# A logarithm from ScalarE's own function, and loads in another order, in a kernel of two wavefront scans and 128 attention images

## What is computed

```python
# L0 and L3: a scan over the cells of a spiral from the middle outwards
def step(g, inp):
    ci, ni, nm, nc = inp                        # cell, its up to 4 neighbours, mask, count
    local = g[:, ci, :]
    neigh = (g[:, ni, :] * nm[None, :, None]).sum(axis=1) / nc
    u = jnp.concatenate([local, neigh], axis=-1)
    y_sc = jnp.tanh(u @ w1 + b1) @ w2 + b2
    return g.at[:, ci, :].set(local + y_sc[:, None] * w_y[None, :]), None

# L1 and L2: attention of the 1024 cells of an image among themselves
q = x @ Wq + bq; k = x @ Wk + bk; v = x @ Wv + bv        # q and k have 16 channels
attn = softmax(q @ k.T)                                   # 1024 x 1024 per image
out = (gamma *) attn @ v + x
```

## Time and profile before

| | |
|---|---|
| runs | 4778.52 us median of 3 (4757.96 to 4780.98) |
| profiled execution | 4771.76 us, span from first to last instruction 4769.6 us |
| mean granted TensorE clock | 0.980 |
| scan 0, attention, scan 1 (by TensorE's first products) | from 13 us, from 816 us, from 3997 us |
| packets under 512 bytes | 443408 of 496962 |

### The profile page before, as it was taken

One profiled execution on the slowest core, in us unless ns is written; L12 is line 12 of the kernel. 1 busy time (PEld: TensorE's weight loads), 2 busy tenths in 40 slices (PEclk: granted clock), 3 DMA queues, 4 the chain that ended last, 5 costly groups with the idle time before them and its releaser, 6 DMA issues.

```text
span 4769.6 us, 56934 instructions
## 1 busy us (share of the span) xinstructions
PE 4486.8 (94%) x17064; PEld 2312.6 (48%) x17064; DVE 3579.9 (75%) x6748; ACT 2850.4 (60%) x5225; POOL 2278.8 (48%) x3972
## 2 busy tenths in 40 slices
PE   5999996999999999999999999999999798999997
PEld 2456754444444444444444444444444343446754
DVE  3888876777777777777777777777777574888876
ACT  1223322777777777777777777777777574223322
POOL 3454431455555555555555555555555455454431
PEclk7999998899999999999999999999999899999998
DMA  9569415111111111111111111111111515379625
GB/s 155 54 74 127 91 31 56 48 57 57 57 57 57 52 53 55 57 57 56 57 57 57 53 54 54 55 57 57 57 57 57 108 53 96 36 75 127 86 53 45
DMA packets 496962, 309.85 MB, mean 65 GB/s; under 512 B 443408, under 2 KB 446736, under 8 KB 496656
## 3 DMA queue, kind: packets, MB, share of 16 engines
q1 hardware_dynamic: 496656, 306.21, 32.7%
HBM read 137.34 MB, written 135.27 MB: 57 GB/s over the span
## 4 chain that ended last, share of the span: by engine, by line
PE 69%; POOL 14%; DVE 6%; issue 6%; SPq 2%; DMA 1%; ACT 1%; DVEq 0%; POOLq 0%; ACTq 0%
PE psum L983 14%; PE psum L925 9%; PE psum L916 8%; PE psum L906 8%; PE psum L954 7%; POOL probs_low L571 7%; PE psum L991 4%; PE psum L967 4%; PE psum L989 3%; PE psum L988 3%; PE psum L1024 3%; PE psum L1002 3%; PE psum L1011 3%; SPq L411 1%; DVE shared L711 1%
## 5 line engine op out<-in xcount | busy, mean ns | idle before, releaser
L571 POOL TENSOR_TENSOR probs_low<-shared,probs_high 128x512 fp32r<-128x512 f32 x1024 | 1307.9, 1277 | 1387.9 <-DVE probs_high L786 1387.9
L748 DVE TENSOR_REDUCE top<-psum 128x1 f32<-128x1024 f32 x1024 | 1253.5, 1224 | 596.8 <-PE psum L967 596.6
L852 ACT ACTIVATE shared<-psum 128x512 f32<-128x512 f32 x2048 | 1108.9, 594 | 376.0 <-PE psum L954 375.8
L857 ACT ACTIVATE psum<-psum,top 128x1024 f32<-128x1024 f32 x1024 | 1114.3, 1088 | 311.0 <-DVE top L748 311.0
L983 PE MATMUL psum<-shared 128*128 128x512 f32 x2048 | 1127.4, 632 | 3.3 <-DVE x L805 0.7
L842 ACT ACTIVATE shared<-psum,b_col 128x320 f32<-128x320 f32 (+10 forms) x744 | 413.3, 566 | 1101.5 <-PE psum L916 1086.5
L562 POOL TENSOR_TENSOR shared<-arena 128x32 f32<-128x32 f32 (+6 forms) x1230 | 570.6, 494 | 870.4 <-PE psum L916 802.6
L988 PE MATMUL psum<-probs_high,v_high 128*128 128x512 f32 x1024 | 813.1, 794 | 0.0
L906 PE MATMUL psum<-arena,w_own 128*128 128x320 f32 (+12 forms) x1672 | 543.3, 453 | 42.2 <-DMA arena<-x_cells 38.3
L916 PE MATMUL psum<-shared,w_sum 128*128 128x320 f32 (+10 forms) x1488 | 529.4, 478 | 42.1 <-POOL shared L562 28.4
L786 DVE CAST probs_high<-shared 128x512 fp32r<-128x512 f32 x1024 | 538.8, 526 | 21.3 <-ACT shared L852 21.3
(11 more groups left out here) (71 smaller groups left out, 4094.8 us busy)
## 6 DMA issues: line engine op xcount, KB each, us to landing
x<-layer_out SPq DMA_DIRECT2D x128, 512.0 KB, 3.2
layer_out<-x SPq DMA_DIRECT2D x128, 512.0 KB, 2.6
q<-q SPq DMA_DIRECT2D x256, 128.0 KB, 2.3
arena<-x_cells SPq DMA_DIRECT2D x8, 1520.0 KB, 10.4
layer_out<-arena SPq DMA_DIRECT2D x8, 1520.0 KB, 19.3
arena<-layer_out SPq DMA_DIRECT2D x8, 1520.0 KB, 10.7
y_cells<-arena SPq DMA_DIRECT2D x8, 1520.0 KB, 20.4
arena<-x_cells SPq DMA_DIRECT2D x4, 1504.0 KB, 18.8
```

The costliest lines, as they stand in the source:

```text
L571: nc.gpsimd.tensor_tensor(probs_low[n % 2][:], probs[u % PROBS], probs_high[n % 2][:], ALU.subtract).then_inc(probs_split, 1)
L748: nc.vector.reduce_max(top[i % 2][:, m:m + 1], rows_ps[m % 2][:], AX_X, negate=True).then_inc(row_max, 1)
L852: nc.scalar.activation(probs[u % PROBS], keys_ps[u % 2], ACT.Exp).then_inc(probs_ready, 1)
L857: nc.scalar.activation(rows_ps[m % 2][:], rows_ps[m % 2][:], ACT.Exp, bias=top[i % 2][:, m:m + 1], accum_out=total[i % 2][:, m:m + 1]).the ...
```

## The change

Five edits.

1. **The logarithm.** ScalarE takes Ln of the sums itself, then exp(-guess) as before; `guess_log` on VectorE is gone. GpSimd forms top - guess, then subtracts (shrink x sum - 1): 6 operations instead of 12. `LOG_TURNS` falls from 11 to 5.
2. **Chunks.** They start at levels 0, 2, 6, 8, 14, 20, 27, 34, 43, 53, 65, 80 and 101, now 13 beside `ENDING`. What isn't a ring's end ends at level 113 (`TAIL` = 114): chunk 12 has 38 cells, and the cells of levels 114 to 121 are counted to `ENDING`, now 28 cells. The arena keeps 512 columns.
3. **Loads by need.** At the start SyncE issues chunks 0, 1, ENDING and 2 of A, the same of B, then 3 to 6 of A and of B. ScalarE's queue issues the weights of both scans.
4. **First images.** During scan 0, behind the store of chunk 11, columns 0 to 957 (`OPEN`) of the images 0 to 3 are loaded; ScalarE copies their last 66 columns from the arena when the scan has ended.
5. **Images read back one by one.** Each image's columns 0 to 482 (`KEPT`) and its `ENDING` chunk are loaded into the arena in two DMAs after its last store, at s == 6 between `place_shift` and `swap_queries`; ScalarE copies those of the last image from x. `first_loads` is gone in both places.

```diff
-WINDOW = 5 * CHUNK - 16
+TAIL = 114
+WINDOW = 452
...
-    first = [0, 2]
-    for lv in range(2, LEVELS):
+    first = [0, 2, 6, 8]
+    for lv in range(8, TAIL):
...
+def wait_loaded(engine, n, g, k, loaded, refilled, last_filled):
+    if n == 0 or k not in FIRST_LOADS:
+        engine.wait_ge(loaded[g][k], 16 * (n + 1))
+    else:
+        engine.wait_ge(refilled[g], 32 * (IMAGES - (g == B)))
+        if g == B:
+            engine.wait_ge(last_filled, 2)
...
+FIRST_LOADS = sorted((k for k in range(NC) if not earlier_tenants(k)),
+                     key=lambda k: (min(FIRST_READ[chunk_cells(k)]), -chunk_size(k) if k else -CELLS))
+KEPT = sum(chunk_size(k) for k in FIRST_LOADS if k != ENDING)
+OPEN = STARTS[CHUNKS[ENDING - 1]]
...
+        def load_first_images():
+            for k in range(ENDING - 1):
+                sp.wait_ge(stored[A][k], 16)
+            for i in range(DEEP):
+                sp.dma_start(x[i][:, 0:OPEN], inner[0][i, :, 0:OPEN]).then_inc(x_in[i], 16)
+
+        def refill(i):
+            if is_job(i) and job_layer(i) == LAYERS - 1 and i < JOBS - 1:
+                g, b = i // (LAYERS * IMAGES), job_image(i)
+                sp.wait_ge(out_stored[i % DEEP], 16 * (i // DEEP + 1))
+                first = PLACES[0]
+                sp.dma_start(arena[:, b, first:first + KEPT], inner[LAYERS][b, :, 0:KEPT]).then_inc(refilled[g], 16)
+                sp.dma_start(arena[:, b, chunk_places_of(ENDING)], inner[LAYERS][b, :, chunk_cells(ENDING)]
+                             ).then_inc(refilled[g], 16)
...
+                if (n, what, k) == (0, "store", ENDING - 2):
+                    load_first_images()
...
-            load_scan_weights(0)
-            first_loads(0, A)
-            load_scan_weights(1)
-            first_loads(0, B)
+            for part in (FIRST_LOADS[:4], FIRST_LOADS[4:]):
+                for g in (A, B):
+                    for k in part:
+                        load(0, g, k)
...
                     if s == 6:
                         place_shift(j + 1)
+                        refill(j - 1)
...
-                if j == EARLY:
-                    first_loads(1, A)
             for b in range(DEEP):
                 sp.wait_ge(out_stored[b], 16 * (JOBS // DEEP))
-            first_loads(1, B)
...
-        def log_sums(i):
+        def shift_values(i):
...
+            pool.wait_ge(guess_ready, i + 1)
+            nc.gpsimd.tensor_tensor(log_sum[:], top[i % 2][:], guess[i % 2][:], ALU.subtract).then_inc(log_turn, 1)
             pool.wait_ge(shrink_ready, i + 1)
+            nc.gpsimd.tensor_tensor(ratio[:], shrink[i % 2][:], total[i % 2][:], ALU.mult).then_inc(log_turn, 1)
+            pool.wait_ge(log_turn, turn + 2)
+            nc.gpsimd.tensor_scalar(ratio[:], ratio[:], -1.0, None, ALU.add).then_inc(log_turn, 1)
+            pool.wait_ge(log_turn, turn + 3)
+            nc.gpsimd.tensor_tensor(ratio[:], log_sum[:], ratio[:], ALU.subtract).then_inc(log_turn, 1)
+            pool.wait_ge(log_turn, turn + 4)
...
         def shrink_sums(i):
             if is_job(i):
+                act.wait_ge(row_summed, MT * (i + 1))
+                nc.scalar.activation(guess[i % 2][:], total[i % 2][:], ACT.Ln).then_inc(guess_ready, 1)
                 act.wait_ge(guess_ready, i + 1)
...
+        def fill_first_images():
+            for i in range(DEEP):
+                for k in (ENDING - 1, ENDING):
+                    nc.scalar.activation(x[i][:, chunk_cells(k)], arena[:, i, chunk_places_of(k)], ACT.Copy
+                                         ).then_inc(x_tail, 1)
+
+        def fill_last_picture():
+            i = JOBS - 1
+            first = PLACES[0]
+            act.wait_ge(out_ready, 2 * i + 1)
+            nc.scalar.activation(arena[:, job_image(i), first:first + KEPT], x[i % DEEP][:, 0:KEPT], ACT.Copy
+                                 ).then_inc(last_filled, 1)
...
             pe.wait_ge(x_in[i % DEEP], 16 * (i // DEEP + 1))
+            if i < DEEP:
+                pe.wait_ge(x_tail, 2 * (i + 1))
```

More of the change, by code:

```diff
@@ L213 @@
 TOP_ROW = 54
-EARLY = JOBS - 12
 LN2 = math.log(2.0)
@@ L340, in network @@
     shrink = [sb(f"shrink{n}", [P, MT]) for n in range(2)]
[L341 to L342 removed]
+    ratio, log_sum = (sb(n, [P, MT]) for n in ("ratio", "log_sum"))
     shift = [sb(f"shift{n}", [P, 2 * MT], F32R) for n in range(2)]
@@ L369, in network @@
     scan_weights_ready = sem("scan_weights_ready")
+    refilled, last_filled, x_tail = [sem(f"refilled{g}") for g in range(GROUPS)], sem("last_filled"), sem("x_tail")
     loaded = [[sem(f"loaded{g}_{k}") for k in range(NC)] for g in range(GROUPS)]
@@ L490, in place_shift @@
                                  shift_row[i % 2][:, cells_of]).then_inc(shift_placed[i % 2], 16)
[L492 to L495, removed]
         def follow(n):
@@ L572, in split_probs @@
                                         ).then_inc(probs_split, 1)
-        def log_sums(i):
+        def shift_values(i):
             if not is_job(i):
                 return
-            s, y, e = total[i % 2], guess[i % 2], shrink[i % 2]
+            turn = LOG_TURNS * i
             high, low = shift[i % 2][:, 0:MT], shift[i % 2][:, MT:2 * MT]
-            turn = LOG_TURNS * i
+            pool.wait_ge(guess_ready, i + 1)
+            nc.gpsimd.tensor_tensor(log_sum[:], top[i % 2][:], guess[i % 2][:], ALU.subtract).then_inc(log_turn, 1)
@@ L793, in low_values @@
                                         ).then_inc(v_ready, 1)
-        def guess_log(i):
-            if is_job(i):
-                dve.wait_ge(row_summed, MT * (i + 1))
-                nc.vector.tensor_scalar(guess[i % 2][:], total[i % 2][:].bitcast(mybir.dt.int32), LN2 / 2.0**23,
-                                        -(127.0 - 0.043) * LN2, ALU.mult, ALU.add).then_inc(guess_ready, 1)
         def output(i, h):
@@ L880, in attention, with load_scan_weights @@
                 values(j + 1, s // 2)
+        def load_scan_weights(n):
+            w1, b1, w2, b2, w_y = scan_weights[n]
+            act.dma_start(w1_own[n][:], w1[0:P, :]).then_inc(scan_weights_in[n], 16)
+            act.dma_start(w1_sum[n][:], w1[P:2 * P, :]).then_inc(scan_weights_in[n], 16)
+            with nc.allow_non_contiguous_dma(reason="small weight columns"):
+                act.dma_start(b1_col[n][:], b1.rearrange("(h p) -> p h", p=P)).then_inc(scan_weights_in[n], 16)
+                act.dma_start(w2_col[n][:], w2.rearrange("(h p) -> p h", p=P)).then_inc(scan_weights_in[n], 16)
+                for h in range(HALVES):
+                    act.dma_start(w2wy[n][h][:], w_y.rearrange("(a c) -> a c", a=1).to_broadcast([P, P])
+                                  ).then_inc(scan_weights_in[n], 16)
+                act.dma_start(wy_col[n][:], w_y.rearrange("(c a) -> c a", a=1)).then_inc(scan_weights_in[n], 16)
+                act.dma_start(b2wy[n][:], b2.to_broadcast([P, 1])).then_inc(scan_weights_in[n], 16)
+        def fill_first_images():
+            for i in range(DEEP):
+                for k in (ENDING - 1, ENDING):
+                    nc.scalar.activation(x[i][:, chunk_cells(k)], arena[:, i, chunk_places_of(k)], ACT.Copy
[6 more added lines that the diff above has]
+                                 ).then_inc(last_filled, 1)
+            act.wait_ge(out_ready, 2 * i + 2)
+            nc.scalar.activation(arena[:, job_image(i), chunk_places_of(ENDING)], x[i % DEEP][:, chunk_cells(ENDING)],
+                                 ACT.Copy).then_inc(last_filled, 1)
+        load_scan_weights(0)
+        load_scan_weights(1)
         act.wait_ge(scan_weights_in[0], 16 * 8)
```

54 lines of the change are left out of this document (14 added, 40 removed).

## The result

| | median us | range | executions |
|---|---|---|---|
| before | 4778.23 | 4757.96 to 4780.98 | 4 |
| after | 4835.37 | 4833.05 to 4838.11 | 4 |

The account below looks back on a forecast made before the run. TensorE was taken as the bound, busy 4486.8 of 4769.6 us, so only its idle time could go. Gains 90 + 27.6 + 19.4 + 27 + 13.7 + 10.1 - 1.3 = 186.5 us gave 4589 us, range 4560 to 4656.

Parts of the forecast that it names:

- The logarithm: Attention stage: TensorE's wait for probs_low goes, gaining 90 us; two extra table loads in all cost 1.3 us, bounds 0 and 4.
- what would show it: Signs listed beforehand; wrong in kind if ScalarE shows hundreds of table loads or TensorE waits for ScalarE in the steady stage.
- rival 1: Attention: logarithm's set lacks the exponential, two table loads per image, 328 us; 5002 us fully exposed, 4838 half; chance 0.08.
- the other terms: Start, first scan to attention, early loads, second scan's start and end: gains of 97.8 us together, without the logarithm.
- The size of the logarithm's gain: Attention: 90 us of the 93.2 us wait for probs_low, 3 us coming back; bounds 45 and 96.
- rival 2: Attention: probs_low's wait is replaced by an equal one for ScalarE or VectorE, a ring of four engines; 4675 us, chance 0.09.
- The start: First scan: B's third chunk load comes seventh in the queue, TensorE starts at 38.7 us, 27.6 earlier; bounds 20 and 36.
- From the first scan to the attention: First images read during the scan's tail gain 20.4 us, less 1 for the swap queued behind stores (bounds 0 and 5): 19.4.
- rival 3: Stage edges: small chunk loads as slow as large ones, swap and stores collide, other terms halve; 4633 us, chance 0.08.
- The early loads: Attention at image 116: seven chunk loads and TensorE's standstill of 25.48 us go; gain 27 us, bounds 24 and 28.
- The start of the second scan: B's sums follow A's at once, so B's product comes 12.7 us earlier, plus 1 us: gain 13.7, lower bound 10.
- The end: After the last update two stores remain instead of four, 12.6 us instead of 22.7: gain 10.1 us, bounds 6 and 13.

Follow-up runs that it names:

- one_set: The kernel after with one table load placed by hand, ahead of the attention, of the set serving exponential and logarithm: 4587.75 us, ratio 0.9593 to before.
- table of stores: No scan or attention, only loads and stores of 4096 short rows, one at a time, at chosen columns and lengths: stores landed in 4.5 to 14.1 us.
- align: The kernel after with an ENDING chunk of 32 cells (992 to 1023) instead of 28, and chunk 12 of 34: 4797.01 us, ratio 1.0031 to before.
- edges_only: The kernel after with the old logarithm (VectorE's guess, GpSimd's 12 operations), so edits 2 to 5 alone: 4718.73 us, ratio 0.9866 to before.
- one_load: one_set with one more table load of the same set per image, ahead of the logarithm: 4667.88 us, ratio 0.9768 to before.

## Why the prediction was wrong, step by step

**The logarithm: the step that failed.** The sentence was: "If the tables are changed only where they must be, there are two more", priced at 1.3 us. There are 256 in the stage, one ahead of each logarithm and one ahead of the exponential behind it, and "what would show it" had named both signs that came: hundreds of table loads, and TensorE waiting for ScalarE. In one_set nothing had to be changed within the stage, so a set for both exists. The profile doesn't name the sets that were picked instead, and no run shows why they were. Price: 247.6 us. I had the case as rival 1, with the right place and mechanism, and gave it 0.08, on the argument that one set already served three functions. That argument says nothing of the fourth. I had also priced its full form too high: 2 x 1.283 fully exposed gave 5002, half exposed 4838. It was 1.93 of 2.57 exposed, against a gain of the logarithm that was larger than assumed; net, edit 1 lost 117 us in the kernel after (4835.37 - 4718.73). That the half-exposed price comes within 3 us of the measured 4835.37 is luck: it gives the logarithm no gain (131.0 measured), exposes too little of the loads, and takes 97.8 us for the other terms, which gave 64.

On this I had set the Trainium skill, "ScalarE activation tables: per-element evaluation and per-set limits", section "Table sets in the compiler and the runtime", by which loads go by the longest run that one set serves. This kernel's trace disagrees: 256 loads in a stage that one set serves from end to end. "ScalarE: Activation LUTs", section "Table sets: the hidden batching unit", promises one load for logarithm and then exponential; its statement that such a set exists is borne out by one_set, the promise is not.

**The size of the logarithm's gain.** 90 us forecast, 131.0 measured without the loads. The bound of 96 came from the wait, as if a wait were all that a stall costs. It was 0.76 us of idle time and 0.25 of bars that no longer overlapped or ran longer per image, 128 x 1.01 = 129. The 3 us that I let come back didn't, and rival 2's equal wait didn't come: TensorE stands 1.9 us in one_set's window of 2700. GpSimd's series ended in time, as worked out.

**The start.** TensorE takes B's first product at 40.41 instead of the forecast 38.7: 25.9 us gained, not 27.6, since GpSimd had its input at 35.36 instead of 33.7; its sums took the 5.0 us forecast. No later load was missed: TensorE has no wait for one in scan 0.

**From the first scan to the attention.** The first projection comes 2.5 us behind the update (766.04 to 768.55), as forecast, but the gain was 4.7 us, not 19.4. The step that failed was "I take off 1 us, bounds 0 and 5" for the swap behind the stores. The swap had a wait of TensorE to itself, 20.4 us, where before it had one of 4.7 (TensorE's waits before):

```profile
PE psum L967 <- DMA q<-q: 5.6, 2, 4.7
```

It grew by 15.7 us, and that is what is missing: 20.4 - 15.7 = 4.7. Of four stores in the queue two are of chunk 12 (cells 958 to 995, both ends off) and two of the last chunk (996 on, one end off), 13.3 and 12.6 us each by the table of stores, 51.8 in all. In the trace they took 48.1 us, from 746.1 to 794.2, and the swaps, issued at 779.4 and 788.5, landed at 792.4 and 794.5. The align run confirms this from the other side. This is a part of rival 3 (the swap and the stores collide), to which I had given 0.08.

**The early loads.** The standstill is gone and no wait took its place; the refills land in 2.4 us (63 of 241.5 KB). In edges_only the attention stage is 23.9 us shorter than before (3146.2 against 3170.1), though its wait for probs_low is 4.2 us longer (97.4 against 93.2), so the standstill was worth some 28, against 27 forecast. By place, edges_only against before is -25.9 in scan 0, -2.3 to the row products, -23.9 in the attention, -12.5 at the start of scan 1 and +8.7 at the end: -55.9 between the two profiled executions (the one of the kernel before was 6.5 us below its median). The forecast for these terms was 97.8.

**The start of the second scan.** 10.4 us between the last attention product and B's product (4064.85 to 4075.23) instead of 22.9: 12.5 gained, 13.7 forecast.

**The end.** 10.1 us gain forecast, 6.2 lost. "Half of it, 12.6 us" took four stores to cost the same and the first two to be done. Chunk 12's, issued at 4782.1, landed at 4798.2 and 4812.6, behind the last update's 4801.7, and the last two at 4823.1 and 4830.2. Before, the last four were two of cells 958 to 1007, with one end off, and two of 1008 to 1023, with none: 10.4 and 4.5 us each by the table of stores, 29.8 in all, and the trace has 24.7 from the first issue to the last landing. The change cut the same 66 cells at 996 instead of 1008, so that both pieces are ragged: 51.8 us by the table, 48.0 in the trace. Sending two of the four earlier, 19.5 us ahead of the update instead of 2.4, didn't make up for it.

With the first step mended, one_set's 4587.75 lies within 2 us of the forecast of 4589. That isn't a confirmation of its sum: +41 of the logarithm stand against -15 of the swap and -16 of the end.

On short stores the Trainium skill, "DMA: Bandwidth & Descriptors", section "Specifications", gives 512 bytes as the size under which the DMA engines read, modify and write. All rows here are 64 to 384 bytes long, so by size alone all would be of one kind; in the table of stores 64- and 128-byte rows at multiples of 64 land in 4.5 us and 380-byte rows off them in 12 to 14.

## What to carry to other kernels

When an edit brings a function to ScalarE that the loop hasn't used, count its table loads as unknown and price both answers; if the joint set isn't sure, place its load by hand ahead of the loop (one instruction was worth 247.6 us here). When a large array is cut into chunks for storing, cut it at multiples of 64 bytes: moving a cut by four cells took 38 us off. And where a critical wait is named for an engine, look for what that engine itself waited for: the same name, GpSimd, stood for two causes here.

## What the hardware showed that I had not expected

- A table load of the set that is loaded already isn't free: 128 of them show the full 1283 ns and cost 80.1 us (one_load).
- A table load overlaps nothing on ScalarE, where ordinary operations overlap by some 0.1 us at each end (2.96 us against 2.64 for the same place).
- A stall of TensorE in the steady stage costs more than the idle time that the profile gives: 0.76 us idle and 0.25 us more, at a granted clock of 1.00 in both windows. At one wait it is 0.77 idle, 0.17 of a bar that nothing overlaps, and 0.10 of a longer first bar (edges_only).
- Stores of 4096 rows take 4.5 to 6.9 us with both ends at multiples of 64 bytes and 10.4 to 14.1 us with one or two ends off; loads show no such step. Whether 32 bytes would do wasn't separated: the one store with a 32-byte end off 64, (966,50), is off at its other end too.
